# A fused Mamba-2 and Hadamard FFN layer on one Trainium2 core: the FFN's high-half copies one tile later on ScalarE, the quads' squares one by one

## The reference

```python
xn = layernorm(x)
x = x + (xn + mamba2(xn, w_in, conv_w, ..., w_out)) + ffn(xn, W1, W2, W3)

# mamba2: 1024 inner columns, 16 heads of 64, state 128
z, xBC, dt = split(xn @ w_in)
xBC = silu(causal_conv4(xBC) + conv_b);  dt = softplus(dt + dt_bias)
y = ssd(xh * dt, dt * A, B, C) + xh * D
y = y * silu(z)
y = y * rsqrt(mean(y * y) + eps) * norm_w
out = y @ w_out

# ffn: 2048 hidden columns
hidden = fwht(silu(xn @ W1.T) * (xn @ W3.T))
out = hidden @ W2.T
```

## Time and profile before

| | us |
|---|---|
| median of 3 runs | 967.65 |
| lowest and highest of them | 966.29, 969.44 |
| the profiled execution's own time | 967.84 |
| its span, first to last instruction | 966.0 |
| PE busy in the span | 936.2 (97%) |
| DVE, ACT, POOL busy | 556.3, 468.6, 191.5 |
| mean clock granted to PE | 0.993 |

### The profile page before, as it was taken

How to read it: one execution, slowest core, us unless ns; L and a number is a source line. 1 busy time by engine, 2 the same in 40 slices (tenths; PEclk the granted TensorE clock), 3 DMA queues, 4 the chain that set the end, 5 groups by cost and what they waited for, 6 DMA issues and landing times.

```text
span 966.0 us, 13499 instructions
## 1 busy us (share of the span) xinstructions
PE 936.2 (97%) x4999; PEld 471.4 (49%) x5000; DVE 556.3 (58%) x956; ACT 468.6 (49%) x962; POOL 191.5 (20%) x146
## 2 busy tenths in 40 slices
PE   8899988989899999999999999999999999999998
PEld 3344454545344445555454445555445445555543
DVE  7876588874534756556532766566451666565421
ACT  6678977745333446255232446365332445554420
POOL 0000333231000104252200103333200102434200
PEclk9999999999999999999999999999999999999999
DMA  9798355443324435535223435446223435255123
GB/s 337 243 348 298 98 192 187 140 131 128 101 77 139 128 107 159 153 82 175 86 69 104 149 98 165 139 101 174 78 76 101 144 106 163 60 151 153 45 77 98
DMA packets 76208, 134.26 MB, mean 139 GB/s; under 512 B 7536, under 2 KB 20464, under 8 KB 74096
## 3 DMA queue, kind: packets, MB, share of 16 engines
q1 hardware_dynamic: 56640, 104.88, 34.2%
q10 hardware_dynamic: 19504, 28.53, 10.0%
HBM read 107.43 MB, written 25.95 MB: 138 GB/s over the span
## 4 chain that ended last, share of the span: by engine, by line
PE 65%; DMA 2%; DVE 2%; ACT 1%; issue 0%; ACTq 0%; DVEq 0%
PE ps L603 44%; PE ps L837 14%; PE ps L799 2%; DMA arena<-cs_rows 2%; PE ps L785 1%; PE ps L791 1%; PE ps L771 1%; DVE arena L1375 0%; ACT arena L1073 0%; PE ps L622 0%; PE ps L641 0%; PE ps L754 0%; DVE arena L1292 0%; DVE arena L1414 0%; PE ps L774 0%
## 5 line engine op out<-in xcount | busy, mean ns | idle before, releaser
L603 PE MATMUL ps<-xh,arena 128*128 128x512 f16 x1592 | 489.1, 380 | 3.4 <-DVE arena L1221 3.3
L603 PE MATMUL ps<-xl,arena 128*128 128x512 f16 x796 | 302.6, 380 | 0.0
L603 PEld LDWEIGHTS ps<-xh,arena 128*128 128x128 f16 x1592 | 158.7, 100 | 191.4 <-issue 7.9
L837 PE MATMUL ps<-arena 128*128 128x512 f16 x768 | 171.1, 379 | 0.0
L1470 POOL TENSOR_TENSOR arena<-arena 128x512 f16<-128x512 f32 x64 | 71.3, 1114 | 384.6 <-ACT arena L981 384.6
L1271 DVE SCALAR_TENSOR_TENSOR arena<-ps,cw,arena 128x511 f32<-128x511 f32 (+2 forms) x120 | 89.5, 748 | 66.6 <-ACT arena L971 64.7
L603 PEld LDWEIGHTS ps<-xl,arena 128*128 128x128 f16 x796 | 78.0, 98 | 88.9 <-issue 3.7
L837 PEld LDWEIGHTS ps<-arena 128*128 128x128 f16 x768 | 74.2, 98 | 91.1 <-issue 5.5
L1287 DVE SCALAR_TENSOR_TENSOR arena<-arena,ps 128x512 f32<-128x512 f32 x64 | 44.0, 687 | 81.1 <-ACT arena L976 81.1
L981 ACT ACTIVATE arena<-arena 128x512 f16<-128x512 f32 x64 | 40.1, 627 | 86.9 <-DVE arena L1292 86.9
L603 PE MATMUL ps<-wo_hi,arena 128*128 128x512 f16 x256 | 78.7, 379 | 2.7 <-DVE wo_lo L1360 1.7
(11 more groups left out here) (179 smaller groups left out, 1080.6 us busy)
## 6 DMA issues: line engine op xcount, KB each, us to landing
arena<-w_parts SPq DMA_DIRECT2D x198, 256.0 KB, 2.6
w_parts<-arena SPq DMA_DIRECT2D x66, 256.0 KB, 2.5
arena<-cs_rows ACTq DMA_DIRECT2D x16, 1024.0 KB, 5.6
arena<-w SPq DMA_DIRECT2D x24, 512.0 KB, 5.1
arena<-ecs_rows ACTq DMA_DIRECT2D x24, 256.0 KB, 6.6
arena<-x ACTq DMA_DIRECT2D x18, 256.0 KB, 3.6
w_mid<-arena SPq DMA_DIRECT2D x8, 512.0 KB, 3.8
arena<-w_mid SPq DMA_DIRECT2D x16, 256.0 KB, 2.7
```

What stands on the lines that cost most here:

```text
L603: ins = nc.tensor.matmul(out_ap, lhs(i, a), rhs(i, c), start=(i == 0 and s == 0), stop=(i == n - 1 and s == 2))
L837: ins = nc.tensor.matmul(bank(t), hw[a][:, i, t * P:(t + 1) * P], w2s[i % W2R][:, d, :], start=(i == 0 and s == 0), stop=(i == JF - 1 and ...
```

## The change

- **The copy.** The copy of token U (L981) leaves the token. It is issued in the token of the tile that follows, behind that tile's tanh (or conv instruction); the copy of the last U of a batch stays where it was. POOL's subtraction stays in token U, so it now waits for that later copy, with everything that stands behind it in POOL's list.
- **The squares.** SQ is numbered by half quads: one square each, at tile places of their own, instead of two in a row. QS of quad 6 moves from place 20 to 18, and its waits change with it.
- **The square of y.** L1109 and its signal go to a new step YS. In batch 0 it stands one place later than Y (10 for 9, 18 for 17, 35 for 34; at chunk 2 none). In the later batches it stands where it was.
- **Batch 0's order.** N and Q of chunk 1 move from place 20 to 21, W of chunk 0 from 18 to 19; that W now waits for seven quad scales (`scale_13`) instead of six.

```diff
-FIRST = ("... F0 C5 F1 SQ0 Z4 F2 C6 F3 QS0 Z5 F4 C7 F5 SQ1 Z6 F6 Z7 F7 QS1 E0 A0").split()
+FIRST = ("... F0 C5 F1 SQ0 Z4 SQ1 F2 C6 F3 QS0 Z5 F4 C7 F5 SQ2 Z6 SQ3 F6 Z7 F7 QS1 E0 A0").split()
...
-             [("SQ", 2, 1), ("QS", 2, 3), ("SQ", 3, 4), ("QS", 3, 7), ("SQ", 4, 8), ("QS", 4, 12), ("SQ", 5, 11), ("QS", 5, 14),
-             ("SQ", 6, 16), ("QS", 6, 20), ("SQ", 7, 20), ("QS", 7, 23)] +
+             [("SQ", n, at) for n, at in enumerate((1, 2, 4, 5, 7, 8, 11, 12, 15, 16, 19, 20), 4)] +
+             [("QS", q, at) for q, at in enumerate((3, 7, 12, 14, 18, 23), 2)] +
...
-              "Y": (9, 17, 26, 34), "N": (12, 20, 28, 37), "Q": (12, 20, 28, 37), "V": (14, 23, 30, 39), "W": (18, 25, 31, 41),
+              "Y": (9, 17, 26, 34), "YS": (10, 18, 26, 35), "N": (12, 21, 28, 37),
+              "Q": (12, 21, 28, 37), "V": (14, 23, 30, 39), "W": (19, 25, 31, 41), "ROW": (15, 24, 31, 40)}
...
                         elif i == 6:
-                            pe.wait_ge(mamba_evac.sem, mamba_evac.at(0, 0))
+                            pe.wait_ge(mean_read.sem, mean_read.at(0, 0))
...
-                            pe.wait_ge(scale_13, 6)
+                            pe.wait_ge(scale_13, 7)
...
+                def hidden_hi(key):
+                    i = key[1]
+                    if i == 0:
+                        act.wait_ge(w2_used.sem, w2_used.at(b, -1))
+                    act.wait_ge(evac.sem, evicted(b, key))
+                    nc.scalar.activation(hid_hi[:, i, :], hs[i % 2], ACT.Copy).then_inc(hid_h.sem, 1)
...
-                    else:
-                        if i == 0:
-                            act.wait_ge(w2_used.sem, w2_used.at(b, -1))
-                        act.wait_ge(evac.sem, evicted(b, key))
-                        nc.scalar.activation(hid_hi[:, i, :], hs[i % 2], ACT.Copy).then_inc(hid_h.sem, 1)
+                    if p > 0 and STREAMS[b][p - 1][0] == "U":
+                        hidden_hi(STREAMS[b][p - 1])
...
                         finish((kind, i))
+                        if POS[b][kind, i] == NT - 1:
+                            hidden_hi((kind, i))
...
                     elif kind == "SQ":
-                        act.wait_ge(d_quad[i], 32)
+                        quad, half_of = divmod(i, 2)
+                        act.wait_ge(d_quad[quad], 32)
...
-                    elif kind == "Y":
+                    elif kind == "YS":
                         if b == 0 and c == 0:
                             act.wait_ge(d_mid[0], 16 * (JF // 4))
                         act.wait_ge(ygate_ok.sem, ygate_ok.at(b, c))
...
                     elif kind == "QS":
                         dve.wait_ge(quad_sums, i + 1)
-                        if i in (4, 6):
-                            dve.wait_ge(pe_tot.sem, pe_tot.at(0, i // 6))
+                        if i == 4:
+                            dve.wait_ge(pe_tot.sem, pe_tot.at(0, 0))
```

More of the change, by code:

```diff
@@ L39 @@
 WARM = (32, 8)
-FIRST = ("B G1S C C0 G1N C1 Z0 DT C2 DTL Z1 C3 Z2 C4 SUM Z3 WOL F0 C5 F1 SQ0 Z4 F2 C6 F3 QS0 Z5 F4 C7 F5 SQ1 Z6 F6 Z7 F7 QS1 E0 A0").split()
+FIRST = ("B G1S C C0 G1N C1 Z0 DT C2 DTL Z1 C3 Z2 C4 SUM Z3 WOL F0 C5 F1 SQ0 Z4 SQ1 F2 C6 F3 QS0 Z5 F4 C7 F5 SQ2 Z6 SQ3 F6 Z7 F7 QS1 E0 A0").split()
 FRONT = "CZCCZCZeCZCZeCPCZCZCPZ"
@@ L50 @@
 STEP_FIRST = {"T": (4, 12, 20, 29), "X": (6, 15, 23, 32), "S": (7, 15, 24, 33), "R": (9, 18, 26, 35), "E": (None, 8, 16, 24),
-              "Y": (9, 17, 26, 34), "N": (12, 20, 28, 37), "Q": (12, 20, 28, 37), "V": (14, 23, 30, 39), "W": (18, 25, 31, 41),
-              "ROW": (15, 24, 31, 40)}
+              "Y": (9, 17, 26, 34), "YS": (10, 18, 26, 35), "N": (12, 21, 28, 37),
+              "Q": (12, 21, 28, 37), "V": (14, 23, 30, 39), "W": (19, 25, 31, 41), "ROW": (15, 24, 31, 40)}
 ES_FIRST = (3, 4, 11, 13, 19, 21, 28, 30)
@@ L63 @@
     "Y": (6, 14, 22, 32),
+    "YS": (6, 14, 22, 32),
     "N": (8, 16, 24, 34),
@@ L1000, in _ @@
                     elif kind == "SQ":
-                        act.wait_ge(d_quad[i], 32)
+                        quad, half_of = divmod(i, 2)
+                        act.wait_ge(d_quad[quad], 32)
                         if i == 0:
                             act.wait_ge(sq_g1, G1_ACT)
-                        elif i == QUADS_EARLY:
+                        elif i == 2 * QUADS_EARLY:
                             act.wait_ge(xt_done.sem, xt_done.at(0, MC - 1))
[L1006 to L1013, removed]
+                        if quad not in (0, QUADS_EARLY):
+                            act.wait_ge(sq_quads, i - 1)
+                        junk = sq_act[quad >= QUADS_EARLY][:, half_of * 2 * TILE:(half_of + 1) * 2 * TILE]
+                        nc.scalar.activation(junk.rearrange("p (s c) -> p s c", s=2), raw_load_view(quad, half_of), ACT.Square,
+                                             accum_out=row_sq[:, SQ_Q + i:SQ_Q + i + 1]).then_inc(sq_quads, 1)
                     elif kind == "F":
```

## The result

| | before | after |
|---|---|---|
| median | 966.97 us (4 runs) | 977.74 us (4 runs) |
| lowest and highest | 965.82, 969.44 | 975.95, 979.18 |
| the profiled execution's own time | 967.84 | 976.72 |
| its span | 966.0 | 974.9 |
| ratio of the medians | | 1.0107, interval 1.0078 to 1.0136 |

The prediction was 966.0 us, range 963.2 to 970.6. The kernel became 10.8 us slower: neither the size nor the sign was right, and 977.74 lies beyond the range.

What follows compares the result with a forecast made beforehand. PE's own work was taken to bound the later batches, while batch 0's idle time hung on DVE and ACT. Gains of 0 at W0, 0.5 at ROW1 and 1.1 later made 1.6 us: 966.0 us, range 963.2 to 970.6.

Steps and rivals of the forecast that it cites:

- YS a tile later: Batch 0, A4 to QS4: moving y's square frees DVE's 1.29 us wait, so w_out's scale is ready 3.7 us earlier.
- The copy, GpSimd's side: Batch 0's A tiles: POOL's subtraction may hold DVE's remainder, 0.87 us each, 0 to 3.5 for four; 1.7 taken.
- L1221's mean: Sign on DVE's remainder to tell DVE's case from POOL's: each lost tie adds 0.87 us to one of its 50.
- likeliest case: The forecast itself, whole kernel: 966.0 us, with 964.7 to 969 given a chance of 0.42.
- second rival: POOL wins the ties and DVE bounds batch 0, 4 us longer less 1.1: 970.6, up to 972; chance 0.21.
- W0: Batch 0, W of chunk 0 a tile later: it waits for QS6's scale; PE keeps nothing with the middle, 1.5 without collisions.
- To chunk 2's N: Batch 0: N1 behind A10 makes yh a tile later, U11's copy leaves ACT's way before ROW1; 0.5 either way.
- head start: Batch 0: w_out's scale ready 3.7 us earlier, at 126.2, shrinking PE's 3.04 us idle before QS4 to 1.6.
- h - 1.9: What PE keeps at W0 in us, h being DVE's head start there: at most 3.4, or 1.7 to 2 with the middle.
- batches 1 to 3: Earlier loads and exponents close the idle stretches before chunk 1's W in batches 1 and 3: 1.1 us gained.
- renamed waits: Rival: ACT's waits go, but batch 0's chain ends as before and later batches idle at Y: 967.6; chance 0.10.
- The copy's waits: Sign on ACT: idle waits of the copy for DVE's product fall from 86.9 us to under 20.

Runs made afterwards that it cites:

- Experiment 9: Only chunk 3's square of y moved from place 34 to 35 in batch 0, on the kernel before; 975.72 us, ratio 1.0083.
- experiment 1: Kernel after with chunk 3's square of y back at place 34 in batch 0; 969.92 us, ratio 1.0011.
- experiment 10: Kernel after with the next batch's normalization at 36 instead of 35, chunk 3's square still at 35; 970.4 us, ratio 1.0031.
- experiment 4: Kernel after with DVE's remainder of batch 0's A tokens made ahead of the gate product; 973.68 us, ratio 1.0058.
- experiment 11: Kernel after with old places for N, Q, W and QS6, chunk 3's square at 34, DVE's A-token remainder before the gate in batch 0; 963.54 us, ratio 0.9964.
- experiment 8: Kernel after with chunk 1's N and Q, chunk 0's W and QS6 at old places and waits, chunk 3's square at 34; 968.14 us, ratio 1.0003.
- experiment 7: Kernel before with the copy moved in batches 1 to 3 only and DVE's A-token remainder before the gate in batch 0; 966.46 us, ratio 0.9983.
- experiment 6: Kernel before with only y's square of chunks 0 and 1 a place later in batch 0, chunk 3's at 34; 967.75 us, ratio 1.0003.
- experiment 2: Kernel after with ACT's copy back in token U in batch 0 alone; 976.16 us, ratio 1.0074.
- experiment 12: As experiment 11, but with the copy in its old place in batch 0, moved in batches 1 to 3 alone; 963.82 us, ratio 0.9963.
- experiment 3: Kernel before with the moved copy alone, in all four batches; 969.4 us, ratio 1.0013.

## Why the prediction was wrong

**The step that failed: "YS a tile later".** The prediction works it out for chunk 0, at A4 and QS4, and for no other chunk. The change moves chunk 3's square too, from 34 to 35, and the prediction has no term for it. There it passes two H steps and the four activations of the next batch's normalization in ACT's list, which wait 6.35 us for DVE (as long as before the change, but then the square stood ahead of them). PE's N of chunk 3 is at 37, two G tiles on, and G tiles are ready work for 2.7 us each; that cover was used up and 5.89 us were left. Experiment 9 shows 8.3 us from this edit alone (8.0 by its ratio), experiment 1 shows 9.3 us when it is undone, experiment 10 7.4 us when only the normalization moves behind it. The trace of before had the price to read: ACT's four L856 start at 254.91, 10.8 us behind the square at 244.15. Of the 8 to 9 us some 1.2 to 1.9 are PE's slow clock behind the stretch.

**Mis-sized: "The copy, GpSimd's side".** The near tie was found, its price of 0.87 was right (0.85 measured, 1.60 against 0.75), and it was said to speak against the change. The middle was chosen between DVE first and GpSimd first, for four A tiles. In the trace there are ten such ties and GpSimd has the start in all of them, so nothing averages out. The prediction's own sign for it, L1221's mean, went from 827 to 975 ns. The decay of chunk 1, put at 0 to 1.9, met a w_out remainder as feared: 2.39 us at 139.61, where an undisturbed one takes 0.75. The likeliest case held 1.7 us in all. The edit that ends the ties gives 4.7 us (experiment 4) and 3.8 (experiment 11 against 8), and little where there are none (experiment 7), so most of it is likely theirs; the two effects of that edit weren't measured apart. The Trainium skill (SBUF — State Buffer, section "SBUF: two separate sides") says that, of a DVE instruction with two SBUF inputs and a GpSimd one that reads SBUF, whichever starts first keeps the shared port pair for its whole length. Taken strictly, that gave this outcome, and the trace agrees with it down to a lead of 0.03 us. The second rival, built on the same outcome, forecast W0 1.1 us later (0.9 measured) and batch 0 longer by 4; at N of chunk 2 it was 4.1. That rival described the first 210 us well, and it had 0.21.

**Mis-sized: "To chunk 2's N".** It was put at 0.5 either way. From W of chunk 1 to N of chunk 2 the kernel after loses 2.2 us (+1.9 to +4.1), nearly all of it at the DVE instruction that GpSimd's sum holds for 2.58 us. The second rival had the cause, the sum behind U11's subtraction, and priced it at 1.1, as a wait for the sum.

**Right: the head start.** QS4 was put at 126.2 with 1.6 idle. It came at 127.10 with 1.43; in experiment 4, without these ties, at 125.96 with 0.43. So the 3.7 us were real, and the ties took 1.1 of them ahead of QS4 (the last, at A4, is 0.85), which the sum had not charged so early.

**Right in kind: W0.** It is preceded by idle time that the seventh scale ends (DVE's L1340 at 165.44, PE at 165.70). The prediction took 0 for it, it cost 0.9: by the formula h - 1.9, about 1 us of head start was left there. The new order as a whole isn't settled better than 0 to 2 us (experiments 1 and 8).

**Right: batches 1 to 3.** The two idle stretches before W of chunk 1 closed and none opened at Y. The forecast was 1.1 us; the time from batch 0's end to the span's is 1.4 shorter (10.3 less 8.9). The renamed waits, as a rival for these batches, are out; in batch 0 experiment 6 shows such a wait that only moves.

**The copy's waits** fell to 9.3 us, under the 20 forecast. This fall of 77.6 us is the change's largest number in the profile. Some 26 us of it lie in batch 0 (with the old copy there alone, experiment 2, the waits are 35.6), and they are worth nothing that can be told: experiments 11 and 12 differ by the copy in batch 0 alone and are equal.

**The range.** The second rival's middle set its top. Added up after the fact: with the missing term of 8 to 9 us on that rival's 970.6, the sum is 978.6 to 979.6, and with the likeliest case's 966.0 it is 974 to 975; the measured 977.74 lies between.

**Open.** How much of experiment 12's gain is the squares', y's square's and the order's wasn't parted further: experiment 7 has the remainder first and the later batches' copies and gives 0.9983, experiment 12 adds the squares and y's square and gives 0.9963, and the intervals overlap. No run makes DVE first by a hair; experiment 4 takes the meeting away as a whole.

## What to carry to other kernels

When a step is moved "by one place" in an in-order schedule, list every instance of it, and for each write what it now stands behind on its engine and what that waits for; the one instance with another kind's wait in front can cost more than all the others give. Waits that vanish from an engine which isn't the bound are no gain: here some 26 us of them bought nothing in batch 0, and swapping two DVE instructions, so that one of them no longer meets GpSimd and runs while DVE would wait anyway, bought 3.8. When two engines that hold each other up are both released by one event, the ties don't average out (here all ten fell to one side): find out who starts first and cost every meeting that way, or change the order so that they don't meet. And when a step is delayed, look for what its engine does behind it, and for what that will now collide with.

## What the runs showed of the hardware

A lead of 0.03 to 0.05 us is enough for GpSimd to hold a DVE remainder until GpSimd's own subtraction is done: 1.60 us against 0.75 in all ten near ties of the kernel after, and the remainder at 120.85 ends 0.55 us behind the subtraction. An instruction of DVE with a single tensor operand is held as well: `tensor_scalar` on 128x512 in f32 takes 2.58 us beside GpSimd's sum and 0.54 alone (2.57 to 2.59 at this place in experiments 1, 3, 8 and 10 too).

PE's granted clock falls to the lower level, 1.2 GHz, behind some idle stretches and not behind others of the same length. Experiments 1 and 10 are the same program until tile place 34, near 245 us. Both stand 3.5 us before chunk 1's Y (3.48 and 3.50). Four stretches of 4 us from 153.50 in experiment 1, with the columns of the earlier trace rows:

```profile
153.50:157.50 4.00, 3.86 (x35) 3.01 (x36) 4.00 (x3) 3.62 (x8) 3.93 (x2) 0.62 0.88 251
157.50:161.50 4.00, 4.00 (x22) 2.04 (x21) 4.00 (x5) 0.55 (x1) 2.24 (x2) 0.95 0.70 114
161.50:165.50 4.00, 1.41 (x8) 0.48 (x7) 3.86 (x10) 2.06 (x4) 0.00 (x0) 1.00 0.81 209
165.50:169.50 4.00, 4.00 (x19) 1.82 (x20) 4.00 (x4) 1.51 (x3) 3.13 (x2) 1.00 1.03 398
```

and the same in experiment 10:

```profile
153.50:157.50 4.00, 3.82 (x41) 2.65 (x42) 4.00 (x4) 3.65 (x8) 3.89 (x2) 1.00 0.88 253
157.50:161.50 4.00, 3.79 (x20) 1.82 (x18) 4.00 (x5) 0.58 (x1) 2.29 (x2) 1.00 0.68 119
161.50:165.50 4.00, 0.00 (x0) 0.02 (x1) 3.86 (x10) 2.01 (x4) 0.00 (x0) 0.99 0.76 204
165.50:169.50 4.00, 3.99 (x11) 1.47 (x12) 4.00 (x4) 1.41 (x3) 3.08 (x2) 0.58 1.04 393
```

In experiment 1 the clock falls at Y (0.62), and the slow work fills a wait that would have come anyway: W0 starts at 165.46 with 2.59 idle and runs at full clock. In experiment 10 it stays full at Y, PE is done earlier, stands 4.22 us, and then falls at W0 (0.58), where PE is the bound: from its first matmul to the next tile's first (24 matmuls) it takes 5.2 us in experiment 1 and 6.8 in experiment 10, 1.6 us more. W0 starts at the same time in both. So an earlier finish in front of a wait can be paid for behind it, and two programs that are equal up to there don't share it.
